# Cross-attention keys of two heads from seven block products in place of eight, and turns in groups on alternating halves of the PSUM banks

## The reference

```python
def _cross_attention(q_in, kv_in, wq, bq, wk, bk, wv, bv, wo, bo, bias_k, bias_v):
    qh = (q_in @ wq + bq).reshape(b, q_len, H, K)          # H = 16 heads, K = 128
    kh = (kv_in @ wk + bk).reshape(b, t, H, K)
    vh = (kv_in @ wv + bv).reshape(b, t, H, K)
    kh = jnp.concatenate([kh, broadcast_to(bias_k, (b, 1, H, K))], axis=1)
    vh = jnp.concatenate([vh, broadcast_to(bias_v, (b, 1, H, K))], axis=1)
    logits = jnp.einsum('bqhk,bthk->bhqt', qh, kh) / sqrt(K)
    weights = jax.nn.softmax(logits, axis=-1)
    return jnp.einsum('bhqt,bthk->bqhk', weights, vh).reshape(b, q_len, H * K) @ wo + bo

h = _layer_norm(x, ln1_scale, ln1_offset); x = x + _cross_attention(h, xf_1, ..1)
h = _layer_norm(x, ln2_scale, ln2_offset); x = x + _cross_attention(h, xf_2, ..2)
```

## Time and profile before

| | |
|---|---|
| median of 3 runs | 1048.21 us (1047.02 to 1049.92) |
| span of the profiled execution | 1047.5 us |
| busy share of the span | TensorE 97%, VectorE 68%, ScalarE 57%, GpSimd 59% |
| granted TensorE clock, whole span | 1.000 |
| chain that ended last | TensorE 73%, GpSimd 11%, VectorE 6%, issue 5%, ScalarE 5% |

### The profile page before, as it was taken

One profiled execution on the slowest core, in us unless ns is written; L12 is line 12 of the kernel. 1 busy time (PEld: TensorE's weight loads), 2 busy tenths in 40 slices (PEclk: granted clock), 3 DMA queues, 4 the chain that ended last, 5 costly groups with the idle time before them and its releaser, 6 DMA issues.

```text
span 1047.5 us, 21298 instructions
## 1 busy us (share of the span) xinstructions
PE 1011.3 (97%) x8275; PEld 908.5 (87%) x8275; DVE 711.9 (68%) x1141; ACT 593.4 (57%) x1296; POOL 614.3 (59%) x617
## 2 busy tenths in 40 slices
PE   7899999999999999999999999999998999989998
PEld 6788888888888999999988999999998888777877
DVE  7997888998266565655567655656556287898760
ACT  5998888797533333222334323332225479999982
POOL 5895476655554443333376445655444388999961
PEclk9999999999999999999999999999999999999999
DMA  9200001000112221202130111101000000000000
GB/s 340 103 2 2 1 2 42 2 1 2 51 61 81 81 82 61 78 25 81 41 104 1 42 40 42 41 21 41 22 10 2 1 1 2 2 1 2 12 12 21
DMA packets 33788, 40.74 MB, mean 39 GB/s; under 512 B 2111, under 2 KB 31257, under 8 KB 32025
## 3 DMA queue, kind: packets, MB, share of 16 engines
q1 hardware_dynamic: 33689, 39.38, 11.3%
HBM read 38.32 MB, written 1.05 MB: 38 GB/s over the span
## 4 chain that ended last, share of the span: by engine, by line
PE 73%; POOL 11%; DVE 6%; issue 5%; ACT 5%; DMA 0%; SPq 0%; POOLq 0%; DVEq 0%; ACTq 0%
PE psum L830 13%; PE psum L715 9%; PE psum L727 9%; PE psum L890 7%; PE psum L844 7%; PE psum L753 5%; PE psum L878 5%; PE psum L858 4%; POOL C tile L1647 3%; PE psum L642 3%; PE psum L743 3%; PE psum L768 2%; PE psum L867 2%; POOL C tile L1653 2%; PE psum L780 1%
## 5 line engine op out<-in xcount | busy, mean ns | idle before, releaser
L1742 POOL TENSOR_TENSOR B tile<-B tile,B rec 128x1024 f32<-128x1024 f32 x32 | 60.7, 1897 | 192.0 <-DVE B rec L1211 192.0
L1653 POOL TENSOR_TENSOR A tile<-A tile,outer rec 128x1024 f32<-128x1024 f32 x48 | 91.0, 1906 | 57.8 <-DVE outer rec L1089 57.7
L1428 ACT ACTIVATE A tile<-A tile,outer min 128x128 f32<-128x128 f32 (+1 forms) x256 | 92.3, 449 | 2.6 <-DVE outer min L1082 2.5
L1343 ACT ACTIVATE B kT<-psum,B bcol 128x1024 f32<-128x1024 f32 x32 | 35.7, 1115 | 98.9 <-PE psum L830 98.9
L1239 DVE TENSOR_TENSOR x_all<-x_all,psum 128x512 f32<-128x512 f32 x64 | 42.6, 683 | 55.2 <-PE psum L890 55.0
L1428 ACT ACTIVATE C tile<-C tile,outer min 128x128 f32<-128x128 f32 x256 | 77.8, 398 | 0.5 <-DVE outer min L1082 0.4
L1499 ACT ACTIVATE B tile<-B max 128x8 f32<-128x8 f32 x32 | 6.9, 215 | 123.4 <-DVE B max L1195 123.4
L971 DVE TENSOR_SCALAR B qT<-psum,B bcol 128x1024 f32<-128x1024 f32 x32 | 41.1, 1283 | 48.8 <-PE psum L830 48.7
L844 PE MATMUL psum<-B v hi,cT hi 128*128 128x256 f32 x256 | 73.5, 287 | 0.3 <-ACT B kT L1343 0.3
L844 PE MATMUL psum<-B v hi,cT lo 128*128 128x256 f32 x256 | 71.9, 281 | 0.0
L844 PE MATMUL psum<-B v lo,cT hi 128*128 128x256 f32 x256 | 71.9, 281 | 0.0
(11 more groups left out here) (294 smaller groups left out, 3470.6 us busy)
## 6 DMA issues: line engine op xcount, KB each, us to landing
weights<-in_weights_c SPq DMA_DIRECT2D x6, 1024.0 KB, 6.3
raw<-in_wq SPq DMA_DIRECT2D x32, 128.0 KB, 2.6
raw<-in_wk SPq DMA_DIRECT2D x32, 128.0 KB, 2.9
raw<-in_wv SPq DMA_DIRECT2D x16, 256.0 KB, 2.8
raw<-in_wo SPq DMA_DIRECT2D x16, 256.0 KB, 2.7
weights<-in_weights_a SPq DMA_DIRECT2D x1, 3072.0 KB, 21.9
weights<-in_weights_a SPq DMA_DIRECT2D x1, 2048.0 KB, 11.3
wide<-in_bias_v SPq DMA_DIRECT2D x2, 1024.0 KB, 9.5
```

Source lines behind the costliest of these rows:

```text
L1428: i = act.activation(of_head, of_head, ACT.Exp, bias=part.min[:, u % 4, h:h + 1], scale=-1.0)
L1653: pool.tensor_tensor(tile(u, ly.nk), tile(u, ly.nk), part.rec[:, u % 4, 0:ly.per].unsqueeze(2).to_broadcast([P, ly.per, ly.nk]), ALU.mult) ...
L1742: pool.tensor_tensor(tv, tv, m.brec[:, h, :].unsqueeze(2).to_broadcast([P, B, S]), ALU.mult).then_inc(s["normalised"].sem, s["normalised"] ...
```

## The change

Three things change together in stage B.

First, the keys of a pair of heads. The 256 x 256 block of `wk` for two heads is cut into four blocks of 128 x 128 (A11, A12 for the first head, A21, A22 for the second), `ctx` into four of 128 x 512 (B11 to B22, feature block x half of the tokens). In place of eight block products, seven are made, over sums of blocks, and added up in the right way; each product still has three passes. The sums of weight blocks S1 to S4 are made by GpSimd for each pair (`cut_forms`), the sums of context blocks T1 to T4 once (`begin_halves`, `make_halves`, `lower_halves`, spread over the first turns of attention 1). ScalarE copies the first product to `kT`; VectorE adds the others with seven operations of 512 columns (`add_products`, `end_products`). `in_seven` says for which pairs: turns 3 to 7 of attention 1 and 1 to 7 of attention 2, 12 pairs. The rest of the keys is projected as before. The last weights of stage C give their room to the sums and are loaded at the end of stage B (`LATE`).

Second, the order within a turn goes by groups: scores of both heads, four output groups, keys of the next pair, values, transposes of both heads, queries of the next pair, weights times values of both heads. The other engines follow.

Third, the banks: turn by turn the scores, keys, transposes and heads take one half of the banks (0 to 3 or 4 to 7), outputs, values and queries the other; turns 0 and 7 have exceptions. Small copies of bias columns on GpSimd (`biases`, `bvcol`) are gone, since the drains read the columns in place.

```diff
-BANKS = {("q", 0): (0, 1), ("k", 0): (2, 3), ("q", 1): (6, 7), ("k", 1): (4, 5)}
-def banks_of(kind, head):
-    return BANKS["q", 1] if (kind, head) == ("k", 2) else BANKS[kind, head % 2]
+def first_set(turn):
+    return turn % 2 * 4
+def other_set(turn):
+    return 4 - first_set(turn)
+FIRST_BANKS = {(1, "q", 0): 0, (1, "k", 0): 2, (1, "q", 1): 6, (1, "k", 1): 4, (2, "q", 0): 0, (2, "k", 0): 4, (2, "q", 1): 6, (2, "k", 1): 4}
+def head_bank(j, kind, head):
+    if head < 2:
+        return FIRST_BANKS[j, kind, head]
+    before = head // 2 - 1
+    first_goes_keys = (kind == "k") == (before > 0)
+    return (first_set(before) if first_goes_keys else other_set(before)) + 2 * (head % 2)
...
+def in_seven(j, turn):
+    return turn > 0 and (j, turn) >= (1, 3)
...
+SEVEN = (("A11", "B11", 0, "product_copied", "P1"), ("S2", "T2", 1, "products_added", "U2"), ("S3", "T3", 2, "products_added", "U3"),
+         ("S1", "T1", 3, "products_added", "C22"), ("A22", "T4", 0, "products_added", "C21"), ("S4", "B22", 1, "products_added", "C12"),
+         ("A12", "B21", 2, "products_added", "C11"))
...
+def scores_bank(turn, h):
+    return first_set(turn) + 2 * h
+def values_bank(turn, n):
+    if turn == 0:
+        return (*AHEAD, 5)[n]
+    return (first_set(turn) if turn == NP_ - 1 else other_set(turn)) + n
+def turned_bank(turn, h):
+    return (first_set(turn) if 0 < turn < NP_ - 1 else other_set(turn)) + 2 * h
 def heads_bank(turn, h):
-    return 6 if turn or h else 2
+    if turn == NP_ - 1:
+        return (6, 0)[h]
+    return first_set(turn) + 2 * h
+def outputs_bank(turn, n):
+    return (0 if turn == NP_ - 1 else other_set(turn + 1)) + n
...
+    def seven_products(j, turn):
+        z, event = head_bank(j, "k", 2 * turn), (j, turn)
...
+        for wt, src, n, drain, what in SEVEN:
+            claim(z + n, drain, (*event, what))
+            for wp, sp in PASSES:
+                i = pe.matmul(bank(z + n), m.block(wt, wp), m.half_of(src, sp), start=(wp, sp) == (0, 0), stop=wp == 1)
+            i.then_inc(s["product_made"].sem, s["product_made"].mark((*event, wt)))
...
             project_heads(j, "q", 1)
-            scores_of(j, 0, 0)
-            scores_of(j, 0, 1)
-            values_of(j, 0, 3, 5)
-            project_heads(j, "q", 2)
-            project_heads(j, "k", 2)
-            turn_weights(j, 0, 0)
-            turn_weights(j, 0, 1)
-            weigh_heads(j, 0, 0)
-            weigh_heads(j, 0, 1)
+            for h in range(2):
+                scores_of(j, 0, h)
+            values_of(j, 0, 3)
+            project_pair(j, "k", 1)
+            project_pair(j, "q", 1)
+            for h in range(2):
+                turn_weights(j, 0, h)
+            for h in range(2):
+                weigh_heads(j, 0, h)
             continue
-        scores_of(j, turn, 0)
-        output(j, turn - 1, 0, 4)
-        output(j, turn - 1, 1, 5)
-        project_heads(j, "q", 2 * turn + 1)
-        project_heads(j, "k", 2 * turn + 1)
-        output(j, turn - 1, 2, 6)
-        output(j, turn - 1, 3, 7)
-        scores_of(j, turn, 1)
+        for h in range(2):
+            scores_of(j, turn, h)
         for n in range(4):
-            values_of(j, turn, n, 4 + n)
-        turn_weights(j, turn, 0)
+            output(j, turn - 1, n)
         if not last:
-            project_heads(j, "q", 2 * turn + 2)
+            project_pair(j, "k", turn + 1)
+        for n in range(4):
+            values_of(j, turn, n)
+        for h in range(2):
+            turn_weights(j, turn, h)
+        if not last:
+            project_pair(j, "q", turn + 1)
         elif j == 1:
             project_heads(2, "k", 0)
         else:
-            two("k", "L3c", 0, 0, 2)
-        weigh_heads(j, turn, 0)
-        turn_weights(j, turn, 1)
-        if not last:
-            project_heads(j, "k", 2 * turn + 2)
-        weigh_heads(j, turn, 1)
+            two("k", "L3c", 0, 0, 4)
+        for h in range(2):
+            weigh_heads(j, turn, h)
...
+    def add_products(j, turn):
+        z, event, made, added = head_bank(j, "k", 2 * turn), (j, turn), s["product_made"], s["products_added"]
+        second = m.col[f"L2_bk{j}"][:, 2 * turn + 1:2 * turn + 2]
+        c11, c12, c21, c22 = (m.kT[k][:, n * BANK:(n + 1) * BANK] for k in range(2) for n in range(2))
+        dve.wait_ge(s["product_copied"].sem, s["product_copied"].at((*event, "P1")))
+        dve.wait_ge(made.sem, made.at((*event, "S2")))
+        dve.tensor_tensor(c12, bank(z + 1), c11, ALU.add).then_inc(added.sem, added.mark((*event, "U2")))
+        dve.wait_ge(made.sem, made.at((*event, "S3")))
+        dve.wait_ge(added.sem, added.at((*event, "U2")))
+        dve.tensor_tensor(c21, bank(z + 2), c12, ALU.add).then_inc(added.sem, added.mark((*event, "U3")))
...
+        dve.wait_ge(made.sem, made.at((*event, "A22")))
+        dve.wait_ge(added.sem, added.at((*event, "C22")))
+        dve.scalar_tensor_tensor(out=c21, in0=bank(z), scalar=second, in1=c21, op0=ALU.add, op1=ALU.add).then_inc(added.sem, added.mark((*event, "C21")))
+        dve.wait_ge(made.sem, made.at((*event, "S4")))
+        dve.scalar_tensor_tensor(out=c12, in0=bank(z + 1), scalar=first, in1=c12, op0=ALU.add, op1=ALU.add).then_inc(added.sem, added.mark((*event, "C12")))
+        dve.wait_ge(made.sem, made.at((*event, "A12")))
+        dve.scalar_tensor_tensor(out=c11, in0=bank(z + 2), scalar=first, in1=c11, op0=ALU.add, op1=ALU.add).then_inc(added.sem, added.mark((*event, "C11")))
...
             queries_of(j, 1)
-            exponentials(j, 0, 0)
-            exponentials(j, 0, 1)
-            divide_by_sum(j, 0, 0)
-            divide_by_sum(j, 0, 1)
+        for h in range(2):
+            exponentials(j, turn, h)
+        if turn:
+            output(j, turn - 1, 0)
+            output(j, turn - 1, 1)
+        divide_by_sum(j, turn, 0)
+        if turn:
+            output(j, turn - 1, 2)
+            output(j, turn - 1, 3)
+        else:
             values_of(j, 0, 3)
-            queries_of(j, 2)
-            weigh_heads(j, 0, 0)
-            weigh_heads(j, 0, 1)
-            continue
-        exponentials(j, turn, 0)
-        output(j, turn - 1, 0, 4)
-        output(j, turn - 1, 1, 5)
-        queries_of(j, 2 * turn + 1)
-        output(j, turn - 1, 2, 6)
-        output(j, turn - 1, 3, 7)
-        divide_by_sum(j, turn, 0)
-        exponentials(j, turn, 1)
-        for n in range(4):
+        shared = not last and in_seven(j, turn + 1)
+        if shared:
+            add_products(j, turn + 1)
+        divide_by_sum(j, turn, 1)
+        if shared:
+            end_products(j, turn + 1)
+        if (j, turn) == (1, 1):
+            make_halves()
+        for n in range(4) if turn else ():
             values_of(j, turn, n)
-        divide_by_sum(j, turn, 1)
         if not last:
             queries_of(j, 2 * turn + 2)
-        weigh_heads(j, turn, 0)
-        weigh_heads(j, turn, 1)
+            queries_of(j, 2 * turn + 3)
+        for h in range(2):
+            weigh_heads(j, turn, h)
...
+        act.copy(m.kT[0][:, 0:BANK], bank(head_bank(j, "k", 2 * turn))).then_inc(s["product_copied"].sem, s["product_copied"].mark((j, turn, "P1")))
...
+    def cut_forms(j, turn):
...
+        pool.tensor_tensor(s1, a21, a22, ALU.add).then_inc(made.sem, made.mark((*event, "S1")))
+        pool.tensor_tensor(s3, a11, a21, ALU.subtract)
+        pool.wait_ge(made.sem, made.at((*event, "S1")))
+        pool.tensor_tensor(s2, s1, a11, ALU.subtract).then_inc(made.sem, made.mark((*event, "S2")))
+        pool.tensor_copy(m.k_cut[0][:, 1:4, :], raw[:, 1:4, :]).then_inc(s["forms_hi"].sem, s["forms_hi"].mark((*event, "raw")))
...
+        pool.tensor_copy(m.forms[0][:, :, :], forms[:, :, :]).then_inc(s["forms_hi"].sem, s["forms_hi"].mark((*event, "made")))
+        pool.wait_ge(s["forms_hi"].sem, s["forms_hi"].at((*event, "made")))
+        pool.tensor_tensor(m.forms[1][:, :, :], forms[:, :, :], m.forms[0][:, :, :], ALU.subtract).then_inc(
+            s["forms_lo"].sem, s["forms_lo"].mark((*event, "made")))
...
+        if turn == 0:
+            cut_pair(j, "k", 1)
+        if not last:
+            cut_pair(j, "q", turn + 1)
         if turn:
-            biases(j, 2 * turn + 1)
-            if not last:
-                biases(j, 2 * turn + 2)
-            cut_qk(j, 2 * turn + 1)
             cut_values(j, turn)
-        else:
-            biases(j, 2)
-            cut_qk(j, 2)
-        divide(j, turn, 0)
-        before = earlier((j, turn), TURNS)
-        if before:
-            pool.wait_ge(s["ot_lo"].sem, s["ot_lo"].at((*before, 1, 1)))
-        pool.tensor_copy(m.bvcol[:, :], m.col[f"L2_bias_v{j}"][:, 2 * turn:2 * turn + 2]).then_inc(
-            s["bias_v_copied"].sem, s["bias_v_copied"].mark((j, turn)))
-        if turn == 0:
-            divide(j, turn, 1)
-        elif not last:
-            cut_qk(j, 2 * turn + 2)
-        elif last and j == 1:
-            biases(2, 0)
-            cut_qk(2, 0)
+        for h in range(2):
```

(9 more changed lines are left out.)

308 lines of the change are left out of this document (207 added, 101 removed).

## The result

| | before | after |
|---|---|---|
| median of 5 runs | 1049.23 us (1047.02 to 1049.92) | 1043.67 us (1041.31 to 1045.29) |
| ratio | | 0.995 (0.9935 to 0.9964) |
| span of the profiled execution | 1047.5 us | 1041.3 us |
| granted TensorE clock, whole span | 1.000 | 0.998 |

The change makes the kernel 0.5% faster; the forecast was 0.64%, 1041.5 us. The median fell inside the range, 2.2 us above the forecast. The span fell by 6.2 us against a forecast of 6.7.

The account below looks back on a forecast made before the run. TensorE, busy 30.00 of 30 us in a steady stretch, was taken as the bound. Terms of -8.3, -1.2, -1.3 and +4.1 gave -6.7 on a span of 1047.5 (median 1048.2): forecast 1041.5 us, range 1037.5 to 1046.5.

Parts of the forecast that it names:

- Term 1: Key products of twelve pairs: seven in place of eight save 0.69 us a pair, -8.3 us.
- Term 4: Turn 0 of both attentions: keys newly wait for bank 5 until VectorE drains it, net +4.1 us.
- Term 2: Order within a turn: grouping halves the slower matmuls after a change of matmul kind, -1.2 us.
- Term 3: Turn 7: three TensorE waits, at head 1's transposes and weights times values, all go, -1.3 us.
- The forecast's own case: The whole kernel comes out as the terms say, 1038 to 1044.5 us by their bounds; chance 62%.
- The edits costed at nothing: VectorE's additions, GpSimd's cuts and sums, late weight loads and attention 2's bias load stay covered, 0 us.
- Seams: Rival, key products: signals and bank claims between products cost 4.8 us, giving 1046.3 us; chance 7%.
- No wait in turn 0: Rival, turn 0: bank 5 is drained in time, +4.1 becomes about -1, giving 1036.5 us; chance 10%.
- The late chain: Rival, VectorE's additions: over 1.1 us late, the sixth and seventh products wait; 1047.5 to 1053.5 us; chance 13%.
- Saving not kept: Rival, the turn: something else binds, or turn 0's waits are twice as long; 1046 to 1050 us; chance 8%.

Follow-up runs that it names:

- experiment 2: The changed kernel's order and banks, but all pairs of keys from eight products as before: 1049.37 us, ratio 1.0011 to the kernel before.
- experiment 8: The changed kernel run again without any edit: 1042.37 us, ratio 0.9944 to the kernel before.
- experiment 1: The changed kernel, with VectorE draining turn 0's last group of values between the two heads' softmax pieces: 1036.86 us, ratio 0.989 to the kernel before.
- experiment 4: The changed kernel with VectorE's first additions put behind head 1's sum, and that sum taken twice: 1058.1 us, ratio 1.0094 to the kernel before.
- experiment 6: The changed kernel with turn 0's last values drained earlier and additions earlier, attention 2's weight-block sums and first-product copy earlier: 1034.56 us, ratio 0.9873 to the kernel before.

## Why the prediction was right, and where it missed

**Term 1 (-8.3) was right.** It gave 0.69 us for the product left out, and experiment 2 measures 0.69, at the density it assumed. In turn 0 of attention 2 the saving is swallowed by the wait for bank 5, whose end doesn't depend on TensorE; the forecast had counted that inside term 4.

**Term 2 (-1.2) was right in size, and partly by luck.** A turn with eight products takes 31.29 us in the new order (turn 1 of attention 1, and experiment 2) against 31.37: 0.08 a turn, 1.1 for 14. The timelines divide it, piece by piece from start to start. Both seams are gone as the term has it: the projections behind transposes take 5.56 us in one piece where two took 5.68, the values 5.65 in place of 5.74. But the transposes of both heads take 1.67 us in one group where two took 1.58, and that loss, which the term lacked, gives half of the gain back. Taking the middle of the bounds happened to cover it.

**Term 3 (-1.3) was right in kind and too small.** None of the waits of the earlier trace rows is left, but turn 7 became 1.25 us shorter in attention 1 and 1.3 in attention 2, with all of the way to the next landmark. Less 0.08 each for the grouping that is 2.4, where the waits alone are 1.3. The step that failed is taking a wait at the length in its brackets. From the transposes of head 0 to the end of the weighing of head 1 the same instructions take 9.06 us before and 7.99 after in attention 1, 7.92 and 6.65 in attention 2, and 7.99 is also what the pieces of attention 1 add up to in a steady turn of the kernel before, where nothing waits (one head's transposes 0.79, the projection 2.85, its weighing 1.78, the other's 0.79 and 1.78). Of these 2.3 us 1.3 are the bracketed waits and 1.0 the slow restarts behind them. The values, which in turn 7 stand directly behind the outputs now, take 5.45 us in place of 5.74, once in each attention: 0.6 that the term lacked. Some 0.3 is lost in other pieces.

**Term 4 (+4.1) had the right mechanism and the right waits.** The waits came where it put them: 2.46 us for 2.7 in attention 1; 0.44 and 2.22 in attention 2, together 2.66 for 3.2, both followed by a slower restart. Between landmarks they cost 1.6 (without the clock) and 2.4, as forecast. The step that failed is the clock: the term costed the matmuls behind the wait at full speed. This is the mis-sized term. In place of +4.1 the two turns 0 cost +5.6 in the profiled execution (3.2 and 2.4) and +6.9 in experiment 8, where both waits had a slow stretch behind them. Over the ten runs of the changed kernel the median is 2.1 us above the one run at full clock (the mean of 1042.48 and 1042.62 is 1042.55, less 1040.49). Not all of the lost clock need lie in turn 0: both stretches of experiment 8 together cost 3.0 us, and three runs without a profile stand 3.2 to 4.8 us above 1040.49.

**The sum.** At full clock the changed kernel stands 1047.4 - 1040.5 = 6.9 us under the kernel before on the same chip, though by a single run; the forecast was 6.7. In the span, 1.6 us of clock and 0.7 at the end stand against 1.1 us more from turn 7 and 0.5 from stage A, so that 6.2 came near 6.7 partly by errors of opposite sign. The prediction's way from the span to the median was off too: each run here takes 1.2 us more than its span (1042.48 for 1041.3), not 0.7, and that half microsecond is part of the miss of 2.2. The forecast's own case was said to reach from 1038 to 1044.5; the bounds that it names add up to 1038.5 to 1046.0.

**The edits costed at nothing held.** The additions start at 10.98 and 11.78 for 11.0 and 11.7, the products at 12.77 and 13.46 for 12.8 and 13.5. GpSimd's sums of weight blocks and their cuts took 5.0 us (in turn 0 of attention 2, in the changed kernel and in experiment 1), the lower end of 5 to 6.5, and no product of a steady turn waits for them.

**The rivals.** *Seams*: ruled out, 21 matmuls with six seams run at 0.2295 us each, the 24 of experiment 2, with two signals in place of seven, at 0.2296. By the Trainium skill (TensorE: Matmul & The Clock Gate, "The cost: per-tile semaphore tail") a serialized increment costs 26.3 ns; an estimate from that for the five more is 0.13 us. No such cost shows inside this stream of 512-column matmuls. *No wait in turn 0*: wrong of this kernel. Experiment 1 comes to it in attention 1, where turn 0 takes 21.39 us, 1.0 less than the same instructions before. In attention 2 it still has the wait of 1.6 us, so that its 1036.9 is near the rival's 1036.5 partly by chance; with nearly all waits gone it is the 1034.6 of experiment 6. *The late chain*: not so here, by the 1.1 us forecast; experiment 4 shows that it costs 1.1 us a turn at 2.2 us of lateness, and would have made the kernel slower. *Saving not kept*: no, the turn of 30.57 us holds all of it.
